# The second MLP product of a two-layer transformer block as three products of scaled fp16 halves

## The chip, the cores and the metric

The kernel runs on one core of one Trainium2 chip, as one launch. The metric is the device time of that core in microseconds (us), 3227.24 as the median of three runs (3226.8 to 3229.04) for the kernel before. The core has five engines that work through instruction queues of their own and meet only at semaphores: TensorE (PE, with its weight loads as PEld), VectorE (DVE), ScalarE (ACT), GpSimd (POOL) and SyncE (SP), which issues the DMAs here.

## The reference

The input x is 4 sequences of 2048 tokens of width 256. First comes an attention stage over the whole sequence, then two layers of local attention and MLP, each stage wrapped in a layer norm and a residual. The change touches the MLP of the layers; `h` is the token-shifted, normalised stream:

```
def _layer(x, wqkv, qs, ksc, wo, lg, lb, w1, b1, w2, b2):
    ...
    x = x + o @ wo
    h = shift_token(x)
    mu = h.mean(-1, keepdims=True)
    var = h.var(-1, keepdims=True)
    h = (h - mu) / jnp.sqrt(var + 1e-05) * lg + lb
    h = h @ w1 + b1
    a, g = jnp.split(h, 2, axis=-1)
    h = a * jax.nn.gelu(g, approximate=False)
    x = x + h @ w2 + b2
    return x
...
for l in range(2):
    x = _layer(x, ...)
```

The hidden width is 682, so `h @ w2` sums over 682 = 5 x 128 + 42 channels and gives 256 columns for each token. All of it is float32 in the reference.

## The kernel before

**Stages.** `phase_a` (the first quarter of the time) does the full attention. `phase_b` does the two layers. It begins with a setup block (L541 to L679) in which SP loads the weights, ScalarE and VectorE split `wqkv`, `wo` and `w1` into a high and a low half, GpSimd scales the rotary tables (L611) and takes a maximum over the partitions (L608), and everyone meets before the main block.

**Slots.** A window is 128 tokens; the two layers together have 128 windows, in 64 pairs. The main block is a software pipeline of slots, one window entering per slot (`slots`, L481; the middle of each layer is a hardware loop of four slots). In slot `s`, an engine runs its part of several stages for different windows: projection and norms of window `s`, scores and softmax of window `s-1`, weighted values and output projection of window `s-2`, the second norm of window `s-3`, and every second slot a piece of the MLP for a pair of windows. In an **even slot** TensorE ends with the first MLP product (L942, 66 matmuls in fp16, already three products of halves); ScalarE applies the gelu (L1013) and VectorE makes `hid` (L1172), six chunks of 128 channels by 256 tokens in float32. In the following **odd slot** TensorE ends with the second MLP product (L953), out of `hid` and `w2` in float32. VectorE adds the residual to it at the start of the next even slot (`layer_output`, L1061).

**What sets the order.** The program text does: each engine's `run` is written out as a fixed order, and an engine that waits for a semaphore holds up all that stands behind. TensorE's order in a slot is: query and key transposes (L845, L852), projections (L867), transposes of the softmax weights (L883), weighted values (L895), scores (L908), output projection (L921), transpose of the next input (L834), and then an MLP product. VectorE's order in an odd slot is: the low halves of query and key (L1096, L1098), second-norm statistics (L1105 to L1109), rotary products (L1039 to L1041, twice, with L1115 and L1118 between), in layer 1 also output statistics (L1068 to L1073), `oT_low` (L1088), eight masked score rows (L1136), `normalise(0)` and `normalise(1)` (L1146, L1149), `xp` (L1160), `normalise(2)`, `keep_hT` (L1024), `normalise(3)`. ScalarE's order there is: L972, L975, the two squares (L979, L981), the copy of v (L984), four copies of transposed weights (L990), the high half of the attention output (L993), eight exponentials (L1000). `oT_low` waits for L993, which waits for L895 of the same slot; the score rows wait for L908; the output projection L921 waits for `oT_low`.

The second product before is one group of float32 matmuls for each window of the pair:

```
pe.wait_ge(hid_ready, HC * (j + 1))
...
for n in range(2):
    for c in range(HC):
        last = nc.tensor.matmul(ps[:, 3, n * D:(n + 1) * D], hid[:, c, n * P:(n + 1) * P], w2[:, ds(layer(2 * j), 1), c, :],
                                start=(c == 0), stop=(c == HC - 1))
last.then_inc(w2_done, 1)
```

## Time and profile before

| | |
|---|---|
| median of three runs | 3227.24 us |
| the profiled execution | 3229.98 us |
| its span, first to last instruction | 3228.2 us |
| PE busy | 3079.6 us, 95% |
| PEld busy | 2590.6 us, 80% |
| DVE busy | 2731.2 us, 85% |
| ACT busy | 1945.7 us, 60% |
| POOL busy | 1872.1 us, 58% |
| PE in the chain that ended last | 71% of the span |

The trace is of one execution. Busy time is an average over phases with different limits, so a stretch of the trace is read for each question. In a row of the timeline the first number is the start, the second the duration, in us from the start of the span; a bracket names the idle time before the row and what ended it. The two MLP products stand in the list of groups as L942 with 4224 matmuls and L953 with 1536, which is 24 for each pair (two records for each float32 matmul in the text).

### The profile page before, as it was taken

What the parts mean: (1) busy time and instruction counts of PE and PEld (TensorE: products, weight loads), DVE (VectorE), ACT (ScalarE), POOL (GpSimd) and SP (SyncE); (2) the same over time, 40 slices, a digit from 0 to 9 for tenths busy, and PEclk for the clock granted to TensorE, in tenths of its full rate; (3) what the DMA queues carried; (4) which work ended last, traced back from release to release, by engine and by line L of the source; (5) the groups of instructions that cost most, each with busy time, mean ns of one, the idle gap of its engine ahead of it and who ended that gap; (6) DMA issues with size and microseconds to landing.
All of it is one profiled execution on the core that took longest, in us unless ns stands there. A gap on an engine that the chain in (4) does not pass through costs nothing.

```text
span 3228.2 us, 86154 instructions
## 1 busy us (share of the span) xinstructions
PE 3079.6 (95%) x25112; PEld 2590.6 (80%) x25112; DVE 2731.2 (85%) x7864; ACT 1945.7 (60%) x4381; POOL 1872.1 (58%) x2307
## 2 busy tenths in 40 slices
PE   6999999994599999999999999999999999999997
PEld 3675848484488888888888888888888888888886
DVE  6878797875688888888888888899999999999995
ACT  5526181622366676666766666666666667676673
POOL 2333434243566666666666666666767767676763
PEclk9999999996799999999999999999999999999999
DMA  1111202015111111111111111122121121211211
GB/s 37 40 59 31 73 19 72 26 63 199 51 45 51 55 49 50 47 53 51 51 49 48 53 49 54 49 52 66 54 61 54 56 64 56 59 54 56 66 56 44
DMA packets 275103, 179.35 MB, mean 56 GB/s; under 512 B 95278, under 2 KB 272914, under 8 KB 274578
## 3 DMA queue, kind: packets, MB, share of 16 engines
q1 hardware_dynamic: 274962, 177.86, 19.0%
q8 instruction: 41, 0.67, 0.1%
q14 instruction: 100, 0.82, 0.1%
HBM read 106.44 MB, written 54.54 MB: 50 GB/s over the span
## 4 chain that ended last, share of the span: by engine, by line
PE 71%; DVE 1%; POOL 1%; issue 1%; ACT 0%; DMA 0%; POOLq 0%; DVEq 0%; SPq 0%; ACTq 0%
PE b_ps L867 16%; PE b_ps L942 14%; PE b_ps L953 10%; PE b_ps L895 7%; PE b_ps L883 7%; PE b_ps L921 6%; PE b_ps L908 6%; PE b_ps L852 2%; PE b_ps L845 2%; PE b_ps L834 1%; POOL b_sq L1188 0%; POOL b_rn L1221 0%; DVE b_probs L1136 0%; DVE b_probs L1149 0%; POOL b_t L1210 0%
## 5 line engine op out<-in xcount | busy, mean ns | idle before, releaser
L1000 ACT ACTIVATE b_probs<-b_probs,b_negmax 128x256 f32<-128x256 f32 x1024 | 505.9, 495 | 78.3 <-DVE b_negmax L1136 77.4
L867 PE MATMUL b_ps<-b_wqkv,b_hT_hi 128*128 128x512 f32 x1536 | 494.5, 403 | 1.0 <-DVE b_hT_lo L1024 1.0
L942 PE MATMUL b_ps<-b_h2T,b_w 128*128 128x256 f16 x4224 | 474.0, 273 | 6.5 <-DMA b_h2T<-b_xh_hl 6.5
L942 PEld LDWEIGHTS b_ps<-b_h2T,b_w 128*128 128x128 f16 x4224 | 414.3, 98 | 55.2 <-DMA b_h2T<-b_xh_hl 6.9
L1188 POOL TENSOR_TENSOR b_sq<-b_sq 128x512 f32<-128x512 f32 (+5 forms) x768 | 418.7, 545 | 61.7 <-ACT b_sq L981 21.6
L1221 POOL TENSOR_TENSOR b_rn<-b_ss_min,b_mhalf 128x16 f32<-128x16 f32 x128 | 377.4, 2948 | 108.8 <-DVE b_ss_min L1048 108.6
L1149 DVE TENSOR_SCALAR b_probs<-b_probs,b_rinv 128x256 f32<-128x256 f32 x1024 | 409.6, 442 | 18.2
L1198 POOL TENSOR_TENSOR b_rstd<-b_var,b_mhalf 128x1 f32<-128x1 f32 x128 | 72.0, 562 | 555.8 <-DVE b_var L1109 555.8
L442 PE MATMUL a_ps<-a_xs,a_E 128*128 128x256 f16 x3072 | 345.2, 273 | 4.1 <-POOL a_xs L233 4.0
L953 PE MATMUL b_ps<-b_w,b_hid 128*128 128x256 f32 x1536 | 342.2, 379 | 1.2 <-DVE b_hid L1172 1.2
L434 PE MATMUL a_ps<-a_xnT 128*128 128x512 f16 x1536 | 339.2, 385 | 3.0 <-ACT a_xnT L382 2.4
L442 PEld LDWEIGHTS a_ps<-a_xs,a_E 128*128 (+1 forms) x3072 | 297.7, 98 | 40.1 <-issue 6.6
L867 PEld LDWEIGHTS b_ps<-b_wqkv,b_hT_hi 128*128 128x128 f32 x1536 | 284.6, 192 | 55.0 <-ACT b_hT_hi L965 1.4
L1136 DVE CUSTOM_DVE_ANT_0 b_probs<-b_ps,b_mask,b_rn 128x256 f32<-128x256 f32 x768 | 324.5, 478 | 0.0
L953 PEld LDWEIGHTS b_ps<-b_w,b_hid 128*128 128x128 f32 x1536 | 286.8, 190 | 37.9 <-DVE b_hid L1172 1.5
L867 PE MATMUL b_ps<-b_wqkv,b_hT_lo 128*128 128x512 f32 x768 | 304.3, 396 | 0.0
L434 PEld LDWEIGHTS a_ps<-a_xnT 128*128 x1536 | 151.8, 99 | 189.2 <-issue 13.0
L990 ACT COPY b_probsT<-b_ps 128x512 f32<-128x512 f32 x512 | 264.0, 611 | 4.7 <-PE b_ps L883 4.6
L1013 ACT ACTIVATE b_gl<-b_ps,b_b,b_w_unit 128x256 f32<-128x256 f32 (+1 forms) x384 | 202.7, 561 | 102.0 <-DVE b_hid L1172 70.0
L895 PE MATMUL b_ps<-b_probsT,b_v 128*64 128x128 f32 x4096 | 251.8, 276 | 0.0
L883 PE MATMUL b_ps<-b_ident_f,b_probs 128*128 128x128 f32 x2048 | 245.9, 273 | 3.5 <-DVE b_xpp L1061 2.2
L883 PEld LDWEIGHTS b_ps<-b_ident_f,b_probs 128*128 128x128 f32 x2048 | 232.7, 142 | 20.1 <-DVE b_xpp L1061 2.5
(133 smaller groups left out, 6507.5 us busy)
## 6 DMA issues: line engine op xcount, KB each, us to landing
b_hx<-xs_dram SPq DMA_DIRECT2D x256, 64.0 KB, 1.9
b_rot<-rot_dram SPq DMA_DIRECT2D x128, 128.0 KB, 2.1
b_xr<-xs_dram SPq DMA_DIRECT2D x128, 128.0 KB, 2.1
xp_dram<-b_xp SPq DMA_DIRECT2D x128, 128.0 KB, 1.7
b_h<-xp_dram SPq DMA_DIRECT2D x256, 64.0 KB, 1.8
a_xn<-in_L_attn_x_dram SPq DMA_DIRECT2D x20, 512.0 KB, 3.8
a_x_res<-in_L_attn_x_dram SPq DMA_DIRECT2D x66, 128.0 KB, 2.1
x_dram<-a_x SPq DMA_DIRECT2D x64, 128.0 KB, 1.7
```

The source lines that it names most:

```text
L434: last = nc.tensor.matmul(ps[:, 4 * u + n, :], xnT[:, a, k, rows], xnT[:, c, k, n * 512:(n + 1) * 512], start=(k == 0 and a == 0 and c == ...
L442: last = nc.tensor.matmul(ps[:, bank, 0:D], E[:, a, j, ds(i * P, P)], xs[:, c, j, :], start=(j == 0 and a == 0 and c == 0), stop=(j == WPB ...
L867: last = nc.tensor.matmul(ps[:, bank, :], hT[:, k, :], wqkv[:, ds(layer(s), 1), part, k, bank * INNER:(bank + 1) * INNER], start=(k == 0 a ...
L883: last = nc.tensor.transpose(ps[:, 3 + p, n * P:(n + 1) * P], probs[:, 2 * p + n // 2, (n % 2) * P:(n % 2 + 1) * P], ident_f[:])
L895: last = nc.tensor.matmul(ps[h * DH:(h + 1) * DH, 7, p * P:(p + 1) * P], v[:, window, (2 * p + h) * DH:(2 * p + h + 1) * DH], probsT[:, p, ...
L942: last = nc.tensor.matmul(ps[:, bank, half * 2 * P:(half + 1) * 2 * P], w1[:, ds(layer(2 * j), 1), wp, k, first:first + P], h2T[:, hp, k, ...
L953: last = nc.tensor.matmul(ps[:, 3, n * D:(n + 1) * D], hid[:, c, n * P:(n + 1) * P], w2[:, ds(layer(2 * j), 1), c, :], start=(c == 0), sto ...
L1000: nc.scalar.activation(probs[:, h, :], probs[:, h, :], ACT.Exp, bias=negmax[:, h:h + 1], scale=-1.0, accum_out=rowsum[:, h:h + 1]).then_in ...
L1136: nc.vector.tensor_tensor_reduce(probs[:, h, :], head_scores(h), which, rn[:, (r - 1) % 2, h:h + 1], ABOVE_ALL, ALU.add, ALU.min, negmax[: ...
L1149: nc.vector.tensor_scalar(probs[:, h, :], probs[:, h, :], rinv[:, h:h + 1], None, ALU.mult).then_inc(probs_ready, 1)
L1188: nc.gpsimd.tensor_tensor(target, target, sq[:, :, width:2 * width], ALU.add).then_inc(ss_halved, 1)
L1221: nc.gpsimd.tensor_tensor(rn[:, r % 2, :], ss_min[:], mhalf[:], ALU.pow).then_inc(rn_ready, 1)
```

## The change

The second product is computed as the first one is: `hid` is multiplied by a power of two and split in a high half (fp16, by ScalarE) and a low half (what is left, fp16, by VectorE), `w2` is split in the setup, and TensorE adds up high x high, high x low and low x high. `PARTS` is ((0, 0), (0, 1), (1, 0)). The result is scaled back where VectorE adds the residual. In the tile `hid_hl` index 0 is the high half and 1 the low one.

```
+HID_PIECES = HC // 2
...
                     if r % 2 == 1 and in_range(2 * j):
-                        pe.wait_ge(hid_ready, HC * (j + 1))
+                        pe.wait_ge(hid_lo, HID_PIECES * (j + 1))
...
                         for n in range(2):
                             for c in range(HC):
-                                last = nc.tensor.matmul(ps[:, 3, n * D:(n + 1) * D], hid[:, c, n * P:(n + 1) * P], w2[:, ds(layer(2 * j), 1), c, :],
-                                                        start=(c == 0), stop=(c == HC - 1))
+                                for a, (hp, wp) in enumerate(PARTS):
+                                    last = nc.tensor.matmul(ps[:, 3, n * D:(n + 1) * D], hid_hl[:, hp, c, n * P:(n + 1) * P],
+                                                            w2[:, ds(layer(2 * j), 1), wp, c, :],
+                                                            start=(c == 0 and a == 0), stop=(c == HC - 1 and a == 2))
...
+                def hid_high(piece, r, pairs, layer):
+                    j = pairs - 2
+                    if r % 2 == 1 and in_range(2 * j):
+                        chunks = slice(2 * piece, 2 * piece + 2)
+                        act.wait_ge(hid_ready, HC * j + chunks.stop)
+                        wait(act, w2_done, j)
+                        nc.scalar.activation(hid_hl[:, 0, chunks, :], hid[:, chunks, :], ACT.Copy, scale=hid_scale[:, ds(layer(2 * j), 1)]).then_inc(hid_hi, 1)
...
+                    hid_high(0, r, pairs, layer)
+                    if in_range(s):
                         act.wait_ge(k_done, s + 1)
...
+                    hid_high(1, r, pairs, layer)
...
+                    hid_high(2, r, pairs, layer)
+                    if in_range(t):
                         act.wait_ge(pv_done, t + 1)
...
-                            nc.vector.tensor_tensor(xpp[:, n, :], ps[:, 3, n * D:(n + 1) * D], xb[:, (r - 6 + n) % 4, :], ALU.add).then_inc(xpp_ready, 1)
+                            nc.vector.scalar_tensor_tensor(xpp[:, n, :], ps[:, 3, n * D:(n + 1) * D], out_unit[:, ds(layer(2 * j), 1)], xb[:, (r - 6 + n) % 4, :],
+                                                           ALU.mult, ALU.add).then_inc(xpp_ready, 1)
...
+                def hid_low(piece, r, pairs, layer):
+                    j = pairs - 2
+                    if r % 2 == 1 and in_range(2 * j):
+                        chunks = slice(2 * piece, 2 * piece + 2)
+                        dve.wait_ge(hid_hi, HID_PIECES * j + piece + 1)
+                        nc.vector.scalar_tensor_tensor(hid_hl[:, 1, chunks, :], hid[:, chunks, :], hid_scale[:, ds(layer(2 * j), 1)], hid_hl[:, 0, chunks, :],
+                                                       ALU.mult, ALU.subtract).then_inc(hid_lo, 1)
...
                     output_stats(pairs - 3, r, layer)
+                    hid_low(0, r, pairs, layer)
+                    hid_low(1, r, pairs, layer)
                     oT_low(s - 2)
...
                     normalise(0)
                     normalise(1)
+                    hid_low(2, r, pairs, layer)
                     t = s - 2
```

In the setup, VectorE now waits for all loads before the maximum is shared, takes the largest absolute value of `w2` (twice 128x1536) and of `b1`, does the low halves of `wqkv` and `wo` ahead of that wait, works out the scales in some ten steps on 128x2 tiles, and makes the low halves of `w2` (twice 128x1536) behind those of `w1`. ScalarE makes the high halves of `w2` in place of scaling it. The mask is loaded in fewer bytes.

On VectorE, the odd slot before, from the second rotary product to the first score rows (L1088 is `oT_low`):

```order
L1039 TENSOR_TENSOR b_t<-b_ps,b_rot 128x512
L1040 TENSOR_TENSOR b_t<-b_ps,b_rot 128x8x32
L1041 TENSOR_TENSOR b_t<-b_ps,b_rot 128x8x32
L1088 TENSOR_TENSOR b_oT<-b_ps,b_oT 128x512
L1128 ISA
L67 REGISTER_ALU
```

and the same place now (L1145 is `hid_low`, L1151 is `oT_low`):

```order
L1093 TENSOR_TENSOR b_t<-b_ps,b_rot 128x512
L1094 TENSOR_TENSOR b_t<-b_ps,b_rot 128x8x32
L1095 TENSOR_TENSOR b_t<-b_ps,b_rot 128x8x32
L1144 REGISTER_ALU
L1145 SCALAR_TENSOR_TENSOR b_hid_hl<-b_hid,b_hid_scale,b_hid_hl 128x512
L1144 REGISTER_ALU
L1145 SCALAR_TENSOR_TENSOR b_hid_hl<-b_hid,b_hid_scale,b_hid_hl 128x512
L1151 TENSOR_TENSOR b_oT<-b_ps,b_oT 128x512
L1193 ISA
```

Two of the three low pieces stand between the rotary products and `oT_low`. The third stands on VectorE behind `normalise(1)` of the same slot, ahead of `xp` (L1226):

```order
L1214 TENSOR_SCALAR b_probs<-b_probs,b_rinv 128x256 x2
L1210 REGISTER_ALU
L1211 RECIPROCAL b_rinv<-b_rowsum 128x2
L1212 REGISTER_ALU
L1214 TENSOR_SCALAR b_probs<-b_probs,b_rinv 128x256 x2
L1144 REGISTER_ALU
L1145 SCALAR_TENSOR_TENSOR b_hid_hl<-b_hid,b_hid_scale,b_hid_hl 128x512
L1223 REGISTER_ALU
L1226 TENSOR_TENSOR b_xp<-b_ps,b_xr 128x256
```

Before, `xp` (L1160) came directly behind the second pair of L1149.

On TensorE, the end of the odd slot now, with the waits (L959 is the output projection, L872 the transpose of the next input, L992 the second MLP product):

```order
L959 MATMUL b_ps<-b_wo,b_oT 128x256 [waits b_v_kept,b_oT_lo]
L959 MATMUL b_ps<-b_wo,b_oT 128x256 x11
L872 MATMUL b_ps<-b_ident_f,b_hx 128x128 [waits b_oT_lo,b_hx_loaded]
L872 MATMUL b_ps<-b_ident_f,b_hx 128x128
L992 MATMUL b_ps<-b_w,b_hid_hl 128x256 [waits b_scores_kept,b_hid_lo]
L992 MATMUL b_ps<-b_w,b_hid_hl 128x256 x35
L883 MATMUL b_ps<-b_ident_f,b_qr 128x128 [waits b_xp_ready,b_v_kept,b_qr_ready]
```

The product stands where it stood; its one wait, ahead of the first of now 36 matmuls, has changed from `hid_ready` to `hid_lo`.

On ScalarE the three high pieces (L1013) stand in the odd slot behind the first square, behind the second square, and behind the four copies of transposed weights (L1042), ahead of the high half of the attention output (L1047):

```order
L1020 CAST b_qT<-b_ps 128x512
L1023 CAST b_kT<-b_ps 128x4x128
L1027 ACTIVATE b_sq<-b_ps 128x512
L1013 ACTIVATE b_hid_hl<-b_hid,b_hid_scale 128x512
L1031 ACTIVATE b_sq<-b_ps 128x512
L1013 ACTIVATE b_hid_hl<-b_hid,b_hid_scale 128x512
L1036 COPY b_v<-b_ps 128x512
```

Nothing else of the main block has moved.

## Rows read from the trace of the kernel before

**Rows 1.** Busy time by stretch, one of layer 0 and one of layer 1.

```profile
core 0: us, PE busy (x) PEld busy (x) DVE busy (x) ACT busy (x) POOL busy (x), PEclk, DMA share, GB/s
1200.00:1400.00 200.00, 200.00 (x1718) 178.52 (x1716) 173.82 (x539) 138.85 (x344) 126.61 (x144) 1.00 0.18 50
2600.00:2800.00 200.00, 200.00 (x1707) 178.38 (x1706) 183.24 (x578) 137.42 (x340) 139.01 (x156) 1.00 0.20 56
```

**Rows 2.** Chain that ended last, in layer 0 (start us, us, what).

```profile
2007.33 7.21 PE b_ps L942 x66
...
2015.41 4.12 PE b_ps L867 x18
2019.53 1.75 PE b_ps L883 x16
...
2024.78 1.63 PE b_ps L921 x12
...
2026.63 5.18 PE b_ps L953 x24
2031.81 0.44 PE b_ps L845 x4
```

**Rows 3.** VectorE's timeline, odd slot of layer 0 (start, duration; idle before, what ended it).

```profile
2023.84 0.69 DVE L1088 TENSOR_TENSOR b_oT<-b_ps,b_oT 128x512 fp32r<-128x512 f32 x1 [1.36 <-ACT b_oT L993]
2024.44 0.47 DVE L1136 CUSTOM_DVE_ANT_0 b_probs<-b_ps,b_mask_now,b_rn 128x256 f32<-128x256 f32 x1
...
2028.68 0.62 DVE L1149 TENSOR_SCALAR b_probs<-b_probs,b_rinv 128x256 f32<-128x256 f32 x2
2029.21 0.42 DVE L1160 TENSOR_TENSOR b_xp<-b_ps,b_xr 128x256 f32<-128x256 f32 x1
```

**Rows 4.** GpSimd's timeline in the same slot.

```profile
2021.92 1.28 POOL L1207 TENSOR_TENSOR b_qr<-b_t 128x512 f32<-128x512 f32 x1
2023.15 1.48 POOL L1188 TENSOR_TENSOR b_sq<-b_sq 128x128 f32<-128x128 f32 x4
2024.59 1.29 POOL L1210 TENSOR_TENSOR b_t<-b_t 128x512 f32<-128x512 f32 x1
2027.12 3.02 POOL L1221 TENSOR_TENSOR b_rn<-b_ss_min,b_mhalf 128x16 f32<-128x16 f32 x1 [1.24 <-DVE b_ss_min L1048]
```

**Rows 5.** ScalarE's timeline in the same slot.

```profile
2019.56 0.59 ACT L984 COPY b_v<-b_ps 128x512 f32<-128x512 f32 x1 [0.77 <-PE b_ps L867]
...
2023.22 0.59 ACT L993 CAST b_oT<-b_ps 128x512 fp32r<-128x512 f32 x1 [1.11 <-PE b_ps L895]
```

**Rows 6.** VectorE's timeline in an odd slot of layer 1.

```profile
2718.67 0.69 DVE L1088 TENSOR_TENSOR b_oT<-b_ps,b_oT 128x512 fp32r<-128x512 f32 x1
...
2724.05 0.42 DVE L1160 TENSOR_TENSOR b_xp<-b_ps,b_xr 128x256 f32<-128x256 f32 x1
```

**Rows 7.** Chain in that slot of layer 1.

```profile
2721.45 5.18 PE b_ps L953 x24
```

**Rows 8.** VectorE's timeline in the setup.

```profile
790.50 3.09 DVE L652 TENSOR_REDUCE p_top<-p_w_f 128x1 f32<-128x2816 f32 x1
...
802.51 11.71 DVE L670 SCALAR_TENSOR_TENSOR b_w<-p_w_f,p_w_scale,b_w 128x2816 f16<-128x2816 f32 x1
...
815.27 3.14 DVE L670 SCALAR_TENSOR_TENSOR b_w<-p_w_f,p_w_scale,b_w 128x2816 f16<-128x2816 f32 x1
```

**Rows 9.** GpSimd's timeline in the setup.

```profile
801.95 9.31 POOL L611 TENSOR_TENSOR p_rot_all<-p_rot_all,p_head_scale 128x4096 f32<-128x4096 f32 x1 [6.76 <-issue]
```

**Rows 10.** TensorE's timeline behind an idle stretch, main block's first slots.

```profile
894.29 0.63 PE L845 MATMUL b_ps<-b_ident_f,b_qr 128*128 128x128 f32 x4 [3.18 <-DVE b_xp L1160]
```

**Rows 11.** TensorE's timeline behind an idle stretch near the end.

```profile
3168.40 3.51 PE L883 MATMUL b_ps<-b_ident_f,b_probs 128*128 128x128 f32 x16 [2.25 <-DVE b_xpp L1061]
```

**Rows 12.** Chain just behind Rows 10, the same 18 matmuls as in Rows 2.

```profile
896.94 6.43 PE b_ps L867 x18
```

**Rows 13.** Busy time and clock (the 0.50) of the stretch of Rows 11.

```profile
3168.40:3171.60 3.20, 3.20 (x15) 3.20 (x16) 1.32 (x5) 1.51 (x3) 1.23 (x2) 0.50 0.68 210
```

More of the change, by code:

```diff
@@ L651, in _ @@
                     dve.wait_ge(w1_gained, KD * (l + 1))
-                    nc.vector.tensor_reduce(top[:, l:l + 1], w1_f[:, l].rearrange("p k n -> p (k n)"), AX.X, ALU.max, apply_absolute_value=True).then_inc(top_ready, 1)
+                    nc.vector.tensor_reduce(top[:, 0, l:l + 1], w1_f[:, l].rearrange("p k n -> p (k n)"), AX.X, ALU.max, apply_absolute_value=True).then_inc(top_ready, 1)
+                dve.wait_ge(loaded, 16 * DMAS)
+                dve.wait_ge(cleared, 4)
+                for l in range(LAYERS):
+                    nc.vector.tensor_reduce(top[:, 1, l:l + 1], w2_f[:, l].rearrange("p c n -> p (c n)"), AX.X, ALU.max, apply_absolute_value=True).then_inc(top_ready, 1)
+                for l in range(LAYERS):
+                    nc.vector.tensor_tensor(b1[:, l, :], ps[:, l, 0:W1_BLOCKS], b1_f[:, l, :], ALU.add).then_inc(bias_added, 1)
+                for l in range(LAYERS):
+                    dve.wait_ge(bias_added, l + 1)
+                    nc.vector.tensor_reduce(top[:, 2, l:l + 1], b1[:, l, :], AX.X, ALU.max, apply_absolute_value=True).then_inc(top_ready, 1)
+                for l in range(LAYERS):
+                    dve.wait_ge(qkv_hi, l + 1)
+                    nc.vector.tensor_tensor(wqkv[:, l, 1], wqkv_f[:, l], wqkv[:, l, 0], ALU.subtract)
+                for l in range(LAYERS):
+                    dve.wait_ge(wo_hi, l + 1)
+                    nc.vector.tensor_tensor(wo[:, l, 1], wo_f[:, l], wo[:, l, 0], ALU.subtract)
                 dve.wait_ge(top_shared, 1)
@@ L656, in _ @@
                 dve.wait_ge(step, 1)
[L657 removed]
+                nc.vector.tensor_scalar(pow2[:].bitcast(I32), top_min[:, 0:2].bitcast(I32), 0x7F800000, None, ALU.bitwise_and).then_inc(step, 1)
                 dve.wait_ge(step, 2)
                 nc.vector.reciprocal(pow2_inv[:], pow2[:]).then_inc(step, 1)
[L660 removed]
@@ L661, in _ @@
-                dve.wait_ge(step, 4)
-                nc.vector.tensor_scalar(w1_scale[:], pow2_inv[:], W1_TOP, None, ALU.mult).then_inc(scale_ready, 1)
-                for l in range(LAYERS):
-                    dve.wait_ge(qkv_hi, l + 1)
-                    nc.vector.tensor_tensor(wqkv[:, l, 1], wqkv_f[:, l], wqkv[:, l, 0], ALU.subtract)
+                nc.vector.tensor_scalar(w1_unit[:], pow2[:, 0], 1.0 / W1_TOP, None, ALU.mult).then_inc(step, 1)
+                nc.vector.tensor_scalar(w2_unit[:], pow2[:, 1], 1.0 / W1_TOP, None, ALU.mult).then_inc(step, 1)
@@ new lines, in _ @@
+                dve.wait_ge(step, 7)
+                nc.vector.tensor_scalar(pre_pow2[:].bitcast(I32), pre_floor[:].bitcast(I32), 0x7F800000, None, ALU.bitwise_and).then_inc(step, 1)
+                dve.wait_ge(step, 8)
+                nc.vector.scalar_tensor_tensor(pre_sq[:], pre_pow2[:], 4.0, pre_pow2[:], ALU.mult, ALU.mult).then_inc(step, 1)
+                dve.wait_ge(step, 9)
+                nc.vector.reciprocal(pre_inv[:], pre_sq[:]).then_inc(step, 1)
+                nc.vector.tensor_scalar(pre_half[:], pre_sq[:], 1.0 / HID_TOP, None, ALU.mult).then_inc(step, 1)
@@ L667, in _ @@
+                dve.wait_ge(step, 11)
+                nc.vector.scalar_tensor_tensor(hid_scale[:], pre_inv[:], HID_TOP, w1_unit[:], ALU.mult, ALU.mult)
+                nc.vector.tensor_tensor(out_unit[:], pre_half[:], w2_unit[:], ALU.mult)
                 dve.wait_ge(scale_ready, 1)
@@ L1167, in run @@
                     if r % 2 == 0 and in_range(2 * j):
-                        wait(dve, w2_done, j)
+                        wait(dve, hid_hi, HID_PIECES * j)
                         for c, bank in enumerate(W1_BANKS):
```

58 lines of the change are left out of this document (35 added, 23 removed).

## The prediction

> **What bounds the kernel now.** I read the busy time by stretches first. In 200 us of layer 0 TensorE is busy for 200.00 us and VectorE for 173.82; in layer 1 it is 200.00 and 183.24 [rows 1]. TensorE sets the pace of the main block and has no hole; VectorE has 26 us of holes in 200, in layer 1 only 17. Then the chain that ended last: in the layers it is TensorE alone, piece after piece [rows 2]. The second MLP product is 5.18 us of a slot [rows 2], so what it saves counts in full, as long as TensorE never has to wait for what the change adds. So the third view is VectorE's timeline in the slot where the product stands [rows 3, 6]: where is VectorE when TensorE reaches the product? TensorE gets there at 2026.63. VectorE is then still in its score rows; it ends the second pair of the normalising steps and starts `xp` at 2029.21, which is 2.58 us later [rows 2, 3]. In layer 1 it is 2724.05 against 2721.45, 2.60 us [rows 6, 7]. The third low piece stands just before `xp`, and the product waits for it.
>
> **The product itself.** Before: 24 records in 5.18 us. Now: 36 fp16 matmuls of 128x256, the form of L942, which takes 7.21 us for 66, that is 0.109 each: 3.93 us. TensorE's work falls by 1.25 us a pair, 80 us over 64 pairs.
>
> **The wait for the third low piece.** A VectorE step of 128x512 with two inputs takes 0.69 us, and the next one starts 0.60 behind its start [rows 3]. The score rows can't start sooner: `oT_low` ends an idle time of 1.36 us on ScalarE's copy, which waited for TensorE's weighted values of that very slot [rows 3, 5]. VectorE is tied to TensorE's place in the slot, so it can't build up a lead. With nothing else late, the third piece ends at 2029.21 + 0.69, some 0.05 pass until TensorE starts, and the product starts 2.58 + 0.74 = 3.32 us later than before. Behind TensorE's wait stands its whole next slot, so the delay is paid in full: 3.32 - 1.25 = 2.07 us longer in layer 0 even if the first two pieces are free.
>
> **The first two low pieces.** They stand ahead of `oT_low`. The room there is 2023.84 minus the end of the rotary product, 1.36 us and a little, and two pieces need 1.20. But they read two tiles in SBUF and GpSimd is at work. In the setup one and the same step, L670, takes 3.14 us alone and 11.71 us when it is issued at 802.51 beside a GpSimd step that runs from 801.95 to 811.26 [rows 8, 9]: 811.26 plus 3.14 is 814.40 and it ended at 814.22, so it stood until GpSimd was through. In the odd slot GpSimd is in `qr` until 2023.20 and then has four short steps in 1.48 us, 0.37 each [rows 4]. I expect: first piece from 2023.20, one short step of GpSimd (0.37), second piece, `oT_low` at 2023.20 + 0.60 + 0.37 + 0.60 = 2024.77, which is 0.93 late. In layer 1 there is no idle time before `oT_low` [rows 6], so both pieces come on top, 1.20 us and about 0.3 of waiting for short steps: 1.5. All of VectorE's slot is late by that, the third piece too; the output projection waits for `oT_low` as well, but that wait lies ahead of the larger one and isn't added.
> Layer 0: 2.07 + 0.93 = 3.0 us a pair. Layer 1: 2.60 + 0.74 + 1.5 - 1.25 = 3.6. Mean 3.3, times 64: 211 us. From both sides: with no waiting for GpSimd at all it is 2.07 and 3.29, 172 us. With the longest plain step, 1.29 us [rows 4], ahead of each piece it is 4.4 and 5.9, 329 us. I take 211, since the neighbours there are the short steps.
>
> **TensorE's clock.** The product starts 3.3 + 0.9 or 1.5 us late, most of it as one hole (in layer 0 4.25 less the 0.7 that TensorE already waits ahead of the output projection: 3.6 us). In this trace TensorE was idle for 2.25 us at the end, and the next 16 transposes took 3.51 us for 1.75, at a granted clock of 0.50, that is 1.2 in place of 2.4 GHz [rows 2, 11, 13]: 1.76 lost. After 3.18 us of idle time the 18 projections took 6.43 for 4.12: 2.3 lost, with a second short idle time between [rows 2, 10, 12]. Now there is such a hole in every pair. Bounds 0 and 2.3 us a pair; I take 1.7, near the row with one hole, and with it 109 us. It falls on the product and the next slot, all on the path.
>
> **ScalarE.** Three pieces of about the size of its 128x512 copies, 0.59 us. The second and third stand where it idles 0.77 and 1.11 us [rows 5]; the first can push the second square by a part of its own length, and GpSimd's sums with it, work that TensorE needs only a slot later, which itself now starts 3 us later. I put it at nothing. If the third one did not fit its hole, `oT_low` would be later by as much; the low pieces cover that too. The scaling in `layer_output` is one operand more in a step of the same size: nothing. GpSimd's own delay by the first two pieces, 2 x 0.60, is hidden in the same way.
>
> **The setup.** L652 takes 3.09 for 2816 elements [rows 8], so the two maxima of `w2` (1536 elements each) take 3.4 us, the two low halves by L670's 3.14 the same, the small steps some 2; the new order also puts the subtractions before the shared maximum, and GpSimd's 9.3 us [rows 9] behind it, where it can again hold VectorE. ScalarE's part changes little. Between 0 and 20; I take 10 us.
>
> **Sum.** 211 + 109 + 10 = 330 us on the profiled execution of 3229.98 (span 3228.2 and 1.8 around it): 3560. It stands 2.7 us over the median of the runs, so 3557; rounded, **3555 us**.
>
> **What a page says against this.** During GpSimd's power step, 2027.12 to 2030.14, VectorE's pair of L1149 took 0.62 us, its usual time [rows 3, 4]: a step that is long on 16 elements does not hold VectorE up. The Trainium skill, in SBUF — State Buffer, section "SBUF: two separate sides", states that a VectorE instruction with two SBUF inputs and a GpSimd instruction that reads SBUF exclude each other for the whole instruction. For L670 the trace agrees. For the power step this trace's pairs do not, though they have one input and not two, so it could still hold for the low piece; that is a rival below.
>
> **Rivals.**
> *The clock stays up.* The wait is there, but TensorE's hole does not cost clock, because work on both sides is dense, while at 894 us the slots had further holes. Against it: 2.25 us was enough once. 3555 - 109 = 3446.
> *The third piece waits for the power step.* With VectorE 0.93 us late, so is the power step: it would run 2028.05 to 2031.07 and the third piece, due at 2030.14, would start 0.93 later. Likewise in layer 1. 64 x 0.93 = 60 us: 3615. For it: L670 and its two inputs. Against it: L1149 beside that very step.
> *Faster: the third piece is in time.* If it is ready by 2026.63, only the saving is left: 3227 - 80 + 10 = 3157. It decides from the point where VectorE comes to the third piece 3.3 us earlier in TensorE's slot than the rows show, say since the product's wait is passed with TensorE's queue still full of older work. What speaks for it is VectorE's holes, 26 us in 200. What speaks against it: the holes lie before `oT_low`, where VectorE waits for TensorE, and none between there and `xp`. Were it half right, with the third piece 1.2 us late, the kernel would come out even.
>
> **How the numbers follow.** Likeliest, wait and clock: 0.62, with its own range 3490 to 3620. Clock stays up: 0.2. Power step: 0.13. The third piece in time: 0.04, and about even: 0.01. The ends: all lower bounds give 3227 + 172 = 3399, all upper ones 3227 + 329 + 147 + 20 = 3723. The range of 8 in 10 takes in the rivals of the clock and the power step and leaves out the corners: 3425 to 3635. A difference under 0.2% (6 us) could not be told from none. Faster 0.04, same 0.01, slower 0.95.
>
> **What the profile of the changed kernel would show.** L992: 36 matmuls a pair, 3.9 us where the clock is full, up to double behind the hole. A wait of TensorE at L992 for VectorE's L1145 of 3 to 4 us in each of some 60 odd slots, the longest entry in the list of waits; PE's share of the span falls from 95% to under 90%. A wait at L959 for L1151 of 0.5 to 1 us in layer 0 and more in layer 1. L1145 of 0.6 to 0.7 us at best, the first two pieces of a slot longer, the third plain. The granted clock at 0.50 behind many of the holes, the mean at about 0.9 in the layers. A pair of slots 4 to 6 us longer, nearly all of it from the odd one's output projection on. Wrong would be: no wait at L992, or the third piece issued before the score rows end; a clock of 1.00 throughout would leave the first rival.

## The result, and the profile after

| | before | changed kernel |
|---|---|---|
| median of the timed runs | 3228.06 us (3226.8 to 3229.04, 4 runs) | 3587.07 us (3585.11 to 3589.63, 4 runs) |
| span of the profiled execution | 3228.2 us | 3587.8 us |
| TensorE busy | 3079.6 us (95%) | 3147.2 us (88%) |
| VectorE busy | 2731.2 us (85%) | 2919.8 us (81%) |

The changed kernel is slower: ratio 1.1113, interval 1.1094 to 1.1132, 359 us more. The forecast was 3555 us with a range of 3425 to 3635; the time lies in it, 32 us above the forecast.

The busy time by stretches, the same two stretches as [rows 1]:

```profile
1200.00:1400.00 200.00, 182.31 (x1601) 158.59 (x1600) 167.38 (x480) 132.09 (x312) 116.09 (x129) 0.96 0.16 45
2600.00:2800.00 200.00, 176.16 (x1510) 151.81 (x1509) 167.69 (x504) 127.13 (x303) 121.80 (x132) 0.94 0.17 49
```

TensorE, without a hole before, now stands for 18 us in 200, in layer 1 for 24. VectorE is busy for a smaller share too (167 against 174 and 183), though it has more to do per pair: it is late, not full. TensorE's waits (waited for: us in total, times, longest):

```profile
PE b_ps L992 <- DVE b_hid_hl L1145: 227.9, 63, 4.6
PE b_ps L959 <- DVE b_oT L1151: 54.4, 63, 2.2
```

These are the two waits that the working asked for, once in each of 63 pairs. In the kernel before each of the two lines waits for VectorE once only: 1.4 us for `oT_low`, 1.2 us for `hid`. The chain that ended last, in one odd slot of layer 0 (it answers to [rows 2]; start, us, what):

```profile
2015.15 0.44 PE b_ps L883 x4
...
2023.86 1.63 PE b_ps L946 x24
...
2030.75 0.76 DVE b_hid_hl L1145
2031.51 0.12 issue
2031.63 5.69 PE b_ps L992 x36
2037.32 0.44 PE b_ps L883 x4
```

Before, this chain was TensorE's alone. Now it leaves TensorE behind the scores, goes through VectorE's score rows and normalisations (left out here) to the third low piece, and comes back at the product. To count how much later the product starts, the timeline is used and not the chain. A piece of the chain begins at the modelled end of the matmul before it, while matmuls overlap: TensorE had issued its next one 0.16 us earlier. Before (L953 is the product, L845 and L852 the first two steps of the next slot):

```profile
2026.47 5.34 PE L953 MATMUL b_ps<-b_w,b_hid 128*128 128x256 f32 x24
2031.65 0.60 PE L845 MATMUL b_ps<-b_ident_f,b_qr 128*128 128x128 f32 x4
2032.09 0.60 PE L852 MATMUL b_ps<-b_ident_f,b_kr 128*128 128x128 f32 x4
```

The slot's first transposes start at 2014.37 before and at 2014.99 now, so the product starts 2026.47 - 2014.37 = 12.10 us into the slot before and 2031.63 - 2014.99 = 16.64 now, which is 4.54 later. VectorE in the same slot, answering to [rows 3]:

```profile
2023.15 2.32 DVE L1145 SCALAR_TENSOR_TENSOR b_hid_hl<-b_hid,b_hid_scale,b_hid_hl 128x512 f16<-128x512 f32 x2
2025.39 0.68 DVE L1151 TENSOR_TENSOR b_oT<-b_ps,b_oT 128x512 fp32r<-128x512 f32 x1
2025.99 0.47 DVE L1201 CUSTOM_DVE_ANT_0 b_probs<-b_ps,b_mask_now,b_rn 128x256 f32<-128x256 f32 x1
...
2030.22 0.61 DVE L1214 TENSOR_SCALAR b_probs<-b_probs,b_rinv 128x256 f32<-128x256 f32 x2
2030.75 0.75 DVE L1145 SCALAR_TENSOR_TENSOR b_hid_hl<-b_hid,b_hid_scale,b_hid_hl 128x512 f16<-128x512 f32 x1
```

and GpSimd beside it, answering to [rows 4]:

```profile
2024.00 2.26 POOL L1254 TENSOR_TENSOR b_sq<-b_sq 128x128 f32<-128x128 f32 x4
2026.21 1.30 POOL L1276 TENSOR_TENSOR b_t<-b_t 128x512 f32<-128x512 f32 x1
2028.74 2.91 POOL L1287 TENSOR_TENSOR b_rn<-b_ss_min,b_mhalf 128x16 f32<-128x16 f32 x1 [1.23 <-DVE b_ss_min L1102]
```

The idle time of 1.36 us ahead of `oT_low` [rows 3] is gone, filled by the two pieces, which need 2.32 us (three in a row take 2.07 in x9 below, where nothing holds them). Counted in both from the chain's start of the slot, `oT_low` starts 2025.39 - 2015.15 = 10.24 us in, and before 2023.84 - 2014.53 = 9.31: 0.93 later. GpSimd's four short steps take 2.26 us in place of 1.48 [rows 4]: the two engines hold each other up. The third piece lies fully inside GpSimd's power step and takes its plain 0.75.

TensorE at the product, and then busy time and clock (third figure from the end) in its first 3.5 us and in the rest:

```profile
2031.63 5.69 PE L992 MATMUL b_ps<-b_w,b_hid_hl 128*128 128x256 f16 x36 [3.61 <-DVE b_hid_hl L1145]
```

```profile
2031.65:2035.15 3.50, 3.50 (x18) 2.53 (x19) 2.99 (x8) 0.00 (x0) 1.77 (x2) 0.53 0.16 52
2035.20:2037.30 2.10, 2.10 (x22) 1.91 (x20) 0.00 (x0) 0.00 (x0) 0.00 (x0) 1.00 0.12 33
```

Behind the hole of 3.61 us the granted clock is 0.53 in the mean of 3.5 us, nearly all of them at the lower level (1.2 GHz), and then 1.00 (2.4 GHz). Here the clock's cost falls on the product alone. In layer 1:

```profile
2699.77 1.47 DVE L1145 SCALAR_TENSOR_TENSOR b_hid_hl<-b_hid,b_hid_scale,b_hid_hl 128x512 f16<-128x512 f32 x2
2701.16 0.68 DVE L1151 TENSOR_TENSOR b_oT<-b_ps,b_oT 128x512 fp32r<-128x512 f32 x1
...
2706.52 0.75 DVE L1145 SCALAR_TENSOR_TENSOR b_hid_hl<-b_hid,b_hid_scale,b_hid_hl 128x512 f16<-128x512 f32 x1
```

```profile
2690.34 0.45 PE b_ps L883 x4
...
2707.40 5.73 PE b_ps L992 x36
```

By the timeline the slot begins at 2690.18, so the product starts 17.22 us in; before it was 2721.29 - 2709.19 = 12.10. That is 5.12 later. `oT_low` is 2701.16 - 2690.34 = 10.82 in by the chain's start of the slot, before 2718.67 - 2709.36 = 9.31 [rows 6]: 1.51 later.

For the experiments one more measure is used: the length of a pair, as the mean of 28 differences between starts of the second product, in layer 0 and in layer 1. It is 36.56 and 36.41 us before, 41.80 and 42.29 after.

### The profile page after: what moved, and what is told of

Its sections match the earlier page's. It is cut to its first block, busy times and chain, and to the rows that moved or that the text cites. A ratio compares the mean times of both kernels' runs of the same rounds, so it can differ in the third digit from the quotient of the medians.

```text
span 3587.8 us, 88553 instructions
## 1 busy us (share of the span) xinstructions
PE 3147.2 (88%) x25880; PEld 2585.8 (72%) x25880; DVE 2919.8 (81%) x8074; ACT 2071.3 (58%) x4573; POOL 1921.5 (54%) x2307
## 4 chain that ended last, share of the span: by engine, by line
PE 56%; DVE 13%; issue 5%; POOL 1%; ACT 1%; DVEq 0%; DMA 0%; POOLq 0%; ACTq 0%; SPq 0%
PE b_ps L905 13%; PE b_ps L980 12%; PE b_ps L992 11%; PE b_ps L933 6%; PE b_ps L921 5%; DVE b_probs L1201 4%; PE b_ps L946 4%; PE b_ps L959 3%; DVE b_hid_hl L1145 2%; DVE b_probs L1214 2%; PE b_ps L883 1%; PE b_ps L890 1%; DVE b_oT L1151 1%; DVE b_negmax L1201 0%; DVE b_t L1093 0%
## 5 line engine op out<-in xcount | busy, mean ns | idle before, releaser
L992 PE MATMUL b_ps<-b_w,b_hid_hl 128*128 128x256 f16 x2304 | 387.6, 350 | 227.9 <-DVE b_hid_hl L1145 227.9
L992 PEld LDWEIGHTS b_ps<-b_w,b_hid_hl 128*128 128x128 f16 x2304 | 283.5, 125 | 329.1 <-issue 207.5
L1254 POOL TENSOR_TENSOR b_sq<-b_sq 128x512 f32<-128x512 f32 (+5 forms) x768 | 467.7, 609 | 60.0 <-ACT b_sq L1031 19.7
L1287 POOL TENSOR_TENSOR b_rn<-b_ss_min,b_mhalf 128x16 f32<-128x16 f32 x128 | 374.7, 2927 | 137.8 <-DVE b_ss_min L1102 137.6
L1214 DVE TENSOR_SCALAR b_probs<-b_probs,b_rinv 128x256 f32<-128x256 f32 x1024 | 430.8, 462 | 18.2
L1020 ACT CAST b_qT<-b_ps 128x512 fp32r<-128x512 f32 x128 | 75.2, 587 | 469.1 <-PE b_ps L883 467.5
L1159 DVE TENSOR_TENSOR b_qT_low<-b_ps,b_qT 128x512 fp32r<-128x512 f32 x128 | 88.4, 691 | 249.1 <-ACT b_qT L1020 240.8
L1042 ACT COPY b_probsT<-b_ps 128x512 f32<-128x512 f32 x512 | 263.7, 609 | 2.8 <-PE b_ps L921 2.7
L959 PE MATMUL b_ps<-b_wo,b_oT 128*128 128x256 f32 x1536 | 216.6, 290 | 54.4 <-DVE b_oT L1151 54.4
```

The lines of the kernel that those rows point to most:

```text
L959: last = nc.tensor.matmul(ps[:, 2, 0:D], oT[:, op, p, :], wo[:, ds(layer(t), 1), wp, p, :], start=(p == 0 and a == 0), stop=(p == HP - 1 a ...
L992: last = nc.tensor.matmul(ps[:, 3, n * D:(n + 1) * D], hid_hl[:, hp, c, n * P:(n + 1) * P], w2[:, ds(layer(2 * j), 1), wp, c, :], start=(c ...
L1042: nc.scalar.copy(probsT[:, p, :], ps[:, 3 + p, :]).then_inc(pT_kept, 1)
L1214: nc.vector.tensor_scalar(probs[:, h, :], probs[:, h, :], rinv[:, h:h + 1], None, ALU.mult).then_inc(probs_ready, 1)
L1254: nc.gpsimd.tensor_tensor(target, target, sq[:, :, width:2 * width], ALU.add).then_inc(ss_halved, 1)
L1287: nc.gpsimd.tensor_tensor(rn[:, r % 2, :], ss_min[:], mhalf[:], ALU.pow).then_inc(rn_ready, 1)
```

## The experiments

Each was timed beside the kernel before (3227 to 3228 us in every comparison). "Slower by" is against that.

| run | time, us | ratio and interval | pair in layer 0, 1, us | product, us |
|---|---|---|---|---|
| changed kernel | 3587.07 | 1.1113 [1.1094, 1.1132] | 41.80, 42.29 | 5.95, 6.25 |
| x1_no_low | 3219.06 | 0.997 [0.9957, 0.9982] | 36.31, 35.97 | 4.09, 4.09 |
| x2b_filler | 3463.16 | 1.073 [1.0712, 1.0747] | 39.89, 40.11 | 4.10, 4.10 |
| x3_by_piece | 3380.28 | 1.0467 [1.045, 1.0485] | 38.60, 38.99 | 4.97, 4.97 |
| x4_third_early | 3352.98 | 1.0384 [1.0366, 1.0401] | 37.95, 38.57 | 4.09, 4.45 |
| x11_third_only | 3492.19 | 1.0815 [1.0797, 1.0833] | 40.59, 40.25 | 5.58, 5.58 |
| x12_first_two | 3287.19 | 1.0182 [1.0165, 1.0199] | 37.24, 37.18 | 4.09, 4.09 |
| x5_spread | 3446.19 | 1.0676 [1.0658, 1.0693] | 39.94, 39.95 | 4.43, 4.43 |
| x7_no_low_floor | 3410.35 | 1.0567 [1.0549, 1.0584] | 39.84, 38.82 | 4.10, 4.10 |
| x8_before_floor | 3389.22 | 1.0506 [1.0488, 1.0523] | 38.63, 39.69 | 5.45, 5.45 |
| x9_behind_scores | 3406.95 | 1.0551 [1.0533, 1.0569] | 39.28, 39.17 | 4.10, 4.22 |
| x10_xp_first | 3408.47 | 1.0556 [1.0538, 1.0573] | 39.07, 39.40 | 4.10, 4.10 |
| x13_third_behind_scores | 3375.98 | 1.0452 [1.0434, 1.0469] | 38.59, 39.00 | 4.09, 4.09 |

The product's time is from the start of its first matmul to the modelled end of its last; it includes waits inside (x3). By this measure the product before takes 5.35 us. From its first start to the start of what follows it is 0.16 to 0.17 less: 5.18 before, 3.93 for 4.09.

**x1_no_low.** Only the product, without the low pieces that VectorE has to make.

```diff
-pe.wait_ge(hid_lo, HID_PIECES * (j + 1))
+pe.wait_ge(hid_hi, HID_PIECES * (j + 1))
-... hid_hl[:, hp, c, n * P:(n + 1) * P] ...
+... hid_hl[:, 0, c, n * P:(n + 1) * P] ...
-hid_low(0, r, pairs, layer)
-hid_low(1, r, pairs, layer)
-hid_low(2, r, pairs, layer)
```

> This kernel leaves the low half of the hidden activations out: VectorE makes no low pieces in the main block, and TensorE runs its 36 fp16 matmuls with the high half throughout, behind ScalarE's high pieces. Theory (the loss is TensorE's wait for VectorE's third low piece, the delay that the first two put on oT_low, and the clock behind the hole): all three go, the product takes 3.9 us at full clock, and the time is 3228 - 80 for the product + 12 for the longer setup = 3160, up to 3180 if GpSimd's chain for the keys is now the one that is late. Rival 1 (36 matmuls with 36 weight loads cost 5.4 to 5.7 us in themselves): 3228 + 64 x 0.4 + 12 = 3265.

Measured 3219.06. Two things follow. The low pieces are the whole loss: 368 us of it hang on three VectorE steps of 0.75 us per pair. But the gain is about a tenth of what the product saves, and this expectation missed by 39 to 59 us. Of the expected saving of 80, setup takes 12, as expected (the first hx transposes start at 835.55 us, before at 823.39). The product saves 5.35 - 4.09 = 1.26 us a pair, and the pair shortens by 0.25 in layer 0 and 0.44 in layer 1. TensorE's waits show the main taker:

```profile
PE b_ps L890 <- POOL b_kr L1289: 39.3, 66, 6.2
```

and the chain that ended last in layer 0 is no longer TensorE's but GpSimd's:

```profile
2008.54 0.34 POOL b_sq L1251
...
2009.49 1.25 POOL b_t L1273
...
2011.98 3.01 POOL b_rn L1284
2015.07 1.04 POOL b_kr L1289
```

With the product shorter, TensorE comes to the transposes of `kr` before GpSimd has multiplied it. GpSimd isn't full (busy 517 us of 800 in layer 0); it is the chain of steps up to `kr` that is long. The trace of the kernel before holds this already, off TensorE's row:

```profile
2030.22 1.04 POOL L1226 TENSOR_TENSOR b_kr<-b_t,b_rn 128x512 f32<-128x512 f32 x1
```

There `kr` is ready at 2031.26 and TensorE starts to transpose it at 2032.09, 0.83 us later. A product shortened by 1.25 us uses up this room.

Of the 39.3 us, 14.2 in 4 waits stand in the kernel before too; new are 25 us, 0.4 a pair. Since an idle time is counted from the modelled end of the matmuls before, the wait costs more than that. From the transposes before `kr` (L845, here L883) to the end of those of `kr`, start to start, a pair takes 0.76 us more than before in layer 0 and 0.65 in layer 1 (means of 28 pairs). The projections take 0.20 and 0.16 us a pair more by the same count. Together this leaves 1.25 - 0.96 = 0.29 and 1.25 - 0.81 = 0.44 us of the saving, where 0.25 and 0.44 were measured.

**x2b_filler.** The hole filled, to see the clock's share.

```diff
-pe.wait_ge(hid_lo, HID_PIECES * (j + 1))
+pe.wait_ge(hid_ready, HC * (j + 1))
 if in_range(s - 1):
     pe.wait_ge(scores_kept, HEADS * (s - 1) + BANK_READ[3])
+for _ in range(28):
+    nc.tensor.matmul(ps[:, 3, 0:D], w1[:, 0, 0, 0, 0:P], w1[:, 0, 0, 0, 0:D], start=True, stop=True)
+pe.wait_ge(hid_lo, HID_PIECES * (j + 1))
```

> In the changed kernel TensorE idles 3.6 us in every odd slot before the second product (line 992), and the granted clock then falls to 0.50 once per pair; the product takes 5.4 to 5.7 us where 36 matmuls at full clock take 3.93. Here 28 matmuls whose result is thrown away (some 3.05 us at full clock, one pass 128x256) stand in that hole, behind the wait for the hidden activations and ahead of the wait for the low pieces; the output is as before. Theory (the fall of the clock is a cost of its own, beside the wait): clock 1.00 throughout the block loop, product 3.9 to 4.0 us, some 1.7 us less in each of 63 pairs, near 3480 us. Rival (the clock's fall costs nothing that the wait would not cost anyway): 3587 within 10 us. If the filler runs past the arrival of the third piece, up to 0.5 us per pair is given back, so 3480 to 3515.

Measured 3463.16: 17 us below the 3480 expected, and 124 us less than the changed kernel with 28 more matmuls per pair. The trace of TensorE there:

```profile
2019.11 3.22 PE L990 MATMUL b_ps<-b_w 128*128 128x256 f16 x28
2022.81 4.11 PE L995 MATMUL b_ps<-b_w,b_hid_hl 128*128 128x256 f16 x36 [0.48 <-DVE b_hid_hl L1148]
```

The hole that remains is 0.48 us, the product takes 4.11, and the granted clock is 1.00 in both stretches of the block loop looked at (1200 to 1400 and 2600 to 2800 us). So the fall of the clock is a cost of its own, 124 us or 1.9 us a pair, and with the clock up the low pieces still cost 3463.16 - 3219.06 = 244 us, by TensorE's two waits.

**x3_by_piece.** The product in order of the chunks, with a wait per piece.

```diff
+nc.tensor.matmul(ps[:, 3, :], zero_h[:], w1[:, 0, 0, 0, 0:2 * D], start=True, stop=False)
-for n in range(2):
-    for c in range(HC):
+for c in range(HC):
+    if c % 2 == 0:
+        pe.wait_ge(hid_lo, HID_PIECES * j + c // 2 + 1)
+    for n in range(2):
```

> TensorE takes the product chunk by chunk for both windows, and waits for each low piece apart: 24 of the 36 matmuls (2.6 us) can run before the third piece. One matmul of zeros over both windows opens the sum (0.2 us). VectorE's and ScalarE's order is that of the changed kernel. Theory: the third piece is as late as before, but behind it stand 12 matmuls, 1.3 us at full clock, and not 36 at a lowered one, 5.5 us: 4.2 us less in each of 63 pairs, 3587 - 265 = 3322; the hole is 0.8 us in layer 0 and the clock stays at 1.00. Rival 2 (VectorE has become the bound by the amount of its work, 1.9 us more a pair, wherever it stands): VectorE's work is the same, so 3587 or little less.

Measured 3380.28, 58 above the expectation. The clock stays up and the wait inside the product falls to 45.1 us in 63 waits. The one for `oT_low` stays (61.2 us, 54.4 in the changed kernel), and new ones stand around it: 22.2 us for `qT_low`, 18.1 for `hT_lo`, all steps of VectorE.

**x4_third_early.** The third piece with the first two, ahead of `oT_low`.

```diff
 hid_low(1, r, pairs, layer)
+hid_low(2, r, pairs, layer)
 oT_low(s - 2)
...
 normalise(1)
-hid_low(2, r, pairs, layer)
```

> Only the third low piece moves, to behind the second one, ahead of oT_low. Theory: the wait at the product goes, and the one at the output projection grows from 0.9 us on average to about 1.8 (0.66 for the piece and a short step of GpSimd). Per pair 1.8 - 1.25 = 0.55 more than before the change: 3228 + 12 + 35 = 3275 if holes of 1.8 us leave the clock alone, 3380 if they lower it as the long one does. Rival 2 (amount of VectorE's work): 3587 or little less. Rival 3 (GpSimd's steps hold all three pieces up, 1.3 us each): 3228 + 12 + 64 x 2.5 = 3400.

Measured 3352.98, the best of the versions that compute the whole result and 234 us better than the changed kernel, yet 78 above what I expected:

```profile
2039.71 3.03 DVE L1145 SCALAR_TENSOR_TENSOR b_hid_hl<-b_hid,b_hid_scale,b_hid_hl 128x512 f16<-128x512 f32 x3
2042.67 0.68 DVE L1151 TENSOR_TENSOR b_oT<-b_ps,b_oT 128x512 fp32r<-128x512 f32 x1
```

Three pieces take 3.03 us, and TensorE's wait for `oT_low` is 104.0 us in 63 waits, 1.65 each, close to the 1.8 that I had expected. So the hold-up beside GpSimd is not what I missed. It is first of all the wait for `kr`: 42.8 us in 57 waits, of which 14.2 stand in the kernel before. x1 has it as well (39.3), so it comes from the shorter product and not from the place of the third piece. In layer 1 the clock falls at times too: the product takes 4.45 us there, and the granted clock is 0.98 from 2600 to 2800 us.

**x11_third_only and x12_first_two.** The two places of the change apart.

```diff
 # x11: no hid_low(0), hid_low(1); chunks 0 to 3 use the high half
+... hid_hl[:, hp if c >= 4 else 0, c, n * P:(n + 1) * P] ...
 # x12: no hid_low(2); chunks 4 and 5 use the high half
+... hid_hl[:, hp if c < 4 else 0, c, n * P:(n + 1) * P] ...
```

> The changed kernel without its first two low pieces (chunks 0 to 3 multiply the high half three times; their low half is left out); the third piece stands where it does in the changed kernel and TensorE waits for it before the whole product. Theory: this piece carries most of the loss. The wait before line 992 (227.9 us there) and the fall of the clock stay, the wait for oT (54 us) goes: 3587 - 54 = 3533 us. Rival (the first two are the larger part, since the third comes behind them): 3400 us or less.

> The changed kernel with the first two low pieces and without the third (chunks 4 and 5 multiply the high half three times; their low half is left out). Theory: what is left is that oT_low, and with it the score rows, the floor step and GpSimd's kr, come 0.9 us (layer 0) to 1.5 us (layer 1) later, in a loop that without low pieces already waits for kr: 3219 + 64 x (0.9 to 1.5) = 3277 to 3315 us, near 3296, and the clock stays 1.00. Rival (the pieces beside GpSimd's halving steps are held and hold these, 2.3 us for two): 3340 us or more.

Over the 3219.06 of x1_no_low, the first two pieces cost 68 us and the third 273, in sum 341 of the 368 that all three cost. x12 came out as expected (3287 for 3277 to 3315), and its waits are those of the theory: 54.6 us for `oT_low`, and 47.5 for `kr` (39.3 in x1 without any low piece). x11 is 41 below the expectation: without the first two pieces the whole slot of VectorE is earlier, so the third is too, and the clock loses less (the product takes 5.58 us, 5.95 and 6.25 with all three). One VectorE step of 0.75 us in the wrong place costs 273 us, since TensorE waits for it 3.5 us a time (217.9 us in 63 waits) and pays some 1.5 us of clock on top (5.58 against 4.09).

**x7_no_low_floor and x8_before_floor.** x1_no_low had shown GpSimd's power step as the bound. It waits for VectorE's floor step on the squared norms, which stands ahead of the seventh score row. Here it stands ahead of the third: x7 without low pieces, x8 the kernel before with this one change.

```diff
 for p in range(HP):
-    if p == HP - 1:
+    if p == 1:
         floor_norms(s)
```

> As the kernel without low pieces (36 matmuls, each of a high half; the low half of the hidden activations is left out), with the floor step on the squared norms ahead of the third score row instead of the seventh, so that GpSimd's power step starts about 0.8 to 1.3 us earlier. Theory (after the shorter product GpSimd's chain to kr bounds the loop and ate the saving): the wait of line 890 for kr, 39 us in 66 waits, goes and the kernel takes 3180 to 3190 us. Rival (something else holds, kr was only the last of several): 3205 to 3219 us.

> The kernel before with nothing changed but the floor step on the squared norms, four score rows earlier as in the run beside it. Theory: TensorE is never idle there and kr is not waited for, so 3228 us within 0.2%. Rival (the floor step is worth something by itself): 3190 to 3215 us.

Both theories and both rivals fell: x8 is 162 us slower than the kernel before, x7 191 us slower than x1_no_low. VectorE and GpSimd in x8, an even slot of layer 0:

```profile
2007.60 1.17 DVE L1048 TENSOR_SCALAR b_ss_min<-b_sq 128x16 f32<-128x16 f32 x1
...
2011.30 0.62 DVE L1149 TENSOR_SCALAR b_probs<-b_probs,b_rinv 128x256 f32<-128x256 f32 x2
2011.83 0.16 DVE L1146 RECIPROCAL b_rinv<-b_rowsum 128x2 f32<-128x2 f32 x1
2012.03 1.47 DVE L1149 TENSOR_SCALAR b_probs<-b_probs,b_rinv 128x256 f32<-128x256 f32 x2
```

```profile
2007.44 1.29 POOL L1210 TENSOR_TENSOR b_t<-b_t 128x512 f32<-128x512 f32 x1
2008.93 3.04 POOL L1221 TENSOR_TENSOR b_rn<-b_ss_min,b_mhalf 128x16 f32<-128x16 f32 x1 [0.19 <-DVE b_ss_min L1048]
2012.05 1.04 POOL L1226 TENSOR_TENSOR b_kr<-b_t,b_rn 128x512 f32<-128x512 f32 x1
```

The floor step has 16 elements. Issued beside GpSimd's L1210, it ends at 2008.77, when L1210 has ended (2008.73): it stood for a whole GpSimd step. The pair of normalisations issued while GpSimd multiplies to `kr` ends at 2013.50 and takes 1.47 in place of 0.62. Over the whole run the floor step takes 1062 ns in the mean against 205 before, and L1149 516 against 442: 128 x 0.86 + 1024 x 0.074 = 186 us more of VectorE's time. In the kernel before the floor step falls behind L1210 and the first three pairs of normalisations start beside the power step, where they take 0.62 us; only the fourth meets `kr` and takes 1.35. That order is worth 162 us.

**x5_spread.** Low pieces ahead of the fifth and the seventh score row and behind the last one, the product of x3, and the floor step ahead of the fifth row.

```diff
 for p in range(HP):
-    if p == HP - 1:
+    if p == HP - 2:
         floor_norms(s)
+    if p >= 2:
+        hid_low(p - 2, r, pairs, layer)
...
+hid_low(2, r, pairs, layer)
```

> The same fp16 product, taken piece by piece (a zero matmul opens the sum, TensorE waits for one piece at a time); no low piece stands ahead of oT_low: pieces 0 and 1 stand among the score rows, piece 2 right behind them, and the small floor step on which GpSimd's power step waits is two rows earlier. The output is unchanged. If the loss lies in where the pieces stand (they hold oT_low, and the third comes after two normalisations), nearly all of it goes: the kernel without low pieces took 3219 us, the zero matmul adds some 0.2 us per pair (14 us), the earlier floor step takes up to 39 us of the wait for kr, and the 2.3 us of the pieces are hidden where TensorE has scores and output projection to do: 3195 to 3260, near 3225 us. Rival (the 2.3 us of VectorE time are themselves the cost, wherever they stand): VectorE is 2.3 us later per pair at hT_lo and the q product waits for it: 3219 + 64 x 2.3 = 3366 us.

Measured 3446.19, 80 us above even the rival. The run changes two things, and x8 shows that the earlier floor step alone is a loss (it takes 1.22 us in the slot at 2037.58), so nothing about the pieces follows from it. The next two runs leave the floor step where it was.

**x9_behind_scores and x10_xp_first.** All three pieces behind the score rows, beside the power step; x10 in addition with the sum `xp` ahead of the normalisations.

```diff
-hid_low(0, r, pairs, layer)
-hid_low(1, r, pairs, layer)
 oT_low(s - 2)
 ...                               # score rows
+hid_low(0, r, pairs, layer)
+hid_low(1, r, pairs, layer)
+hid_low(2, r, pairs, layer)
```

> The same fp16 product piece by piece (a zero matmul opens the sum), all three low pieces right behind the score rows, none ahead of oT_low, and the floor step on the norms left where it was. The output is unchanged. Theory (the cost lies where the pieces stand): oT_low and the score rows are as without low pieces, the pieces run beside GpSimd's power step, which does not hold them; behind them the first two normalisations meet GpSimd's multiplication to kr and are held by about 1 us, and the sum xp, for which TensorE's next transposes wait, is 2.3 to 3.3 us later than without low pieces. TensorE's product starts behind the first piece, so it ends some 1.0 us later than without low pieces, and xp holds it some 1 us more: 3219 + 64 x (1.0 to 2.0) = 3285 to 3350, near 3310 us; clock 1.00. Rival (the 2.3 us are lost wherever they stand): 3366 us or more.

> As the run beside it, with the sum xp ahead of all normalisations and hT_lo behind the first one. The output is unchanged. Theory: TensorE waits for xp and hT_lo no longer; what is left is the late first piece, 3219 + 64 x 1.0 = 3283 us, if the four normalisations, now some 3 us later, are still in time for the transposes of the next slot. Rival: VectorE has no room left (83 to 92% busy before, plus 2.3 us per 36 us), the late normalisations hold TensorE's transposes of probs or the hidden activations of the even slot: 3320 us or more, no better than the run beside it.

Measured 3406.95 and 3408.47: x9 is 57 above the end of its range, and x10 gains nothing on it, as its rival had it. In x9:

```profile
2043.78 2.07 DVE L1150 SCALAR_TENSOR_TENSOR b_hid_hl<-b_hid,b_hid_scale,b_hid_hl 128x512 f16<-128x512 f32 x3
2045.77 0.15 DVE L1217 RECIPROCAL b_rinv<-b_rowsum 128x2 f32<-128x2 f32 x1
2045.96 1.44 DVE L1220 TENSOR_SCALAR b_probs<-b_probs,b_rinv 128x256 f32<-128x256 f32 x2
```

```profile
2043.21 2.91 POOL L1292 TENSOR_TENSOR b_rn<-b_ss_min,b_mhalf 128x16 f32<-128x16 f32 x1 [0.92 <-DVE b_ss_min L1107]
2046.20 1.04 POOL L1297 TENSOR_TENSOR b_kr<-b_t,b_rn 128x512 f32<-128x512 f32 x1
```

The pieces pass the power step without a hold (0.69 each), the normalisation behind them meets `kr` and is held (1.44), both as expected. But TensorE is through with the matmul of zeros at 2042.9 and the first piece ends at 2044.5: 110.7 us of waiting in 63 waits, and it waits for `hT_lo` (34.9) and `qT_low` (21.4) as well.

**x13_third_behind_scores.** x3 with the third piece ahead of the normalisations.

> As the run by piece (zero matmul opens the sum, one wait per piece, 3380 us), with the third low piece right behind the score rows instead of behind the first two normalisations, beside GpSimd's power step. The output is unchanged. Theory (the third piece is late by the two normalisations ahead of it): the wait of the second product, 45.1 us in 63 waits in the run by piece, goes, and nothing else comes later than there, since the same steps stand ahead of xp and hT_lo: 3380 - 45 = 3335 us. Rival (the normalisations, now 0.75 us later, meet GpSimd's multiplication to kr, which holds them, so the sum xp and hT_lo come later): no gain or a loss, 3380 us or more.

Its edit moves one line, `hid_low(2, r, pairs, layer)`, from behind `normalise(1)` to behind the score rows. Measured 3375.98, 4 us better than x3 where 45 were expected; the pairs are the same to 0.01 us. The wait in the product is gone, 36 matmuls run through in 4.09 us:

```profile
PE b_ps L961 <- DVE b_oT L1156: 60.9, 63, 1.5
...
PE b_ps L907 <- DVE b_hT_lo L1083: 37.5, 55, 1.0
PE b_ps L892 <- POOL b_kr L1297: 29.5, 60, 6.2
```

In its place are waits right behind the product, for `hT_lo` (37.5 us, 18.1 in x3) and `kr` (29.5, 14.2 in x3). That is the rival. The waits point to what sets the pace once the third piece is in time: the way through `oT_low`, the score rows, the floor step, the power step and `kr`, and VectorE's own steps up to `hT_lo`. TensorE can wait in the product or behind it. No run takes one of these two ways out by itself.

## Why the prediction came out right

- **The bound and the place of the wait.** Right. 63 waits at line 992 for the third low piece, one a pair, of 3.6 us in the mean; TensorE's share of the span went from 95% to 88%.
- **The product, 3.93 us.** Right: by start to start it is 5.18 us before and 3.93 in x1. The 4.09 to 4.11 us of the table and of x2b's row count the tail of the last matmul as well, as the 5.35 before does.
- **The third piece, 3.32 us late.** Right in kind, a little small: the product started 4.54 us later in layer 0 and 5.12 in layer 1, forecast were 3.32 + 0.93 = 4.25 and 2.60 + 0.74 + 1.5 = 4.84. Of the missing 0.29 and 0.28, 0.16 is a misreading: I took 2026.63, where the product's piece of the chain begins [rows 2], for the moment when TensorE gets to it, and that was 2026.47. Another 0.08 is in the slot's projections.
- **The first two pieces, 0.93 and 1.5.** Measured 0.93 and 1.51. x12 shows them by themselves: pairs longer by 0.93 (36.31 to 37.24) and 1.21 us. In layer 1 the size was right for a partly wrong reason: I counted 0.3 us of waiting by VectorE, and there it was mostly GpSimd that was held (L1145 1.47 for two there, 2.32 in layer 0).
- **The clock, 1.7 us a pair, 109 us.** Right in kind, a little small: x2b measured 124 us. I had taken the row with one hole of 2.25 us [rows 11]; the hole here is 3.61. The 1.7 was a choice between 0 and 2.3, so its closeness is in part luck.
- **The first rival (the clock stays up, 3446).** x2b is the case made real, at 3463.
- **The power step as a hold-up (3615).** Refuted: the third piece lies inside L1287 with 0.75 us, and three in a row in x9 with 0.69 each. For this the Trainium skill states, in SBUF — State Buffer, section "SBUF: two separate sides", that VectorE with two SBUF inputs and GpSimd reading SBUF exclude each other for the whole instruction. For GpSimd's 128x128 steps the trace agrees (two pieces in 2.32 us, four GpSimd steps in 2.26 for 1.48), for the power step it does not; the measurement decides.
- **Faster, from a third piece in time (3157).** Its condition was tried and its price was wrong. x13 has the piece in time and takes 3376, and even without any low piece the kernel takes 3219, not 3157. The working treated TensorE as the only engine with a claim on the pair's length, and so it booked the product's saving in full. x1 shows that the way to `kr` allowed little less than 36 us a pair. The forecast did not suffer: with the product 4.5 us late, TensorE comes to `kr` after it is ready, and the changed kernel has no more of this wait (14.1 us in 4) than the kernel before. The working says of GpSimd's sums that TensorE needs them only a slot later, but it put no number on how early they were.
- **ScalarE at nothing, setup at 10.** The high pieces take some 0.7 us (0.71 and 0.77 in the slot at 2015); x1 has them all and shows no wait for them but one of 2.7 us. Setup took 12. Its L700, 2 elements wide, stood for 8.73 us beside a GpSimd step on 128x4096, as the forecast had it for a step in this place.

The 32 us that the forecast was short are, per pair and roughly: 0.16 by the misreading above, 0.2 in the clock (x2b), and 0.16 in the projections (4.20 against 4.12 in the chain, twice), 33 us over 64 pairs. Why the projections take 0.08 us more I did not find; x1 and x2b have the 4.20 as well.

The sum of the loss as the runs give it: 124 us is the clock (x2b), 83 the difference to x3, where TensorE takes the pieces one by one, and 4 the third piece's place once that is so (x13); 157 remain up to x1. Some 14 of them are the matmul of zeros that x3 and x13 have and x1 has not (0.22 us a pair). The rest goes with the 2.3 us of VectorE work per pair, and no place that was tried made it cheap (x4, x9, x10 and x13 lie between 134 and 189 over x1); whether another place would is open. The saving of the product gives back 9. No version that makes the low halves on VectorE came near the kernel before; the best is x4 with 3353. Whether GpSimd or the idle part of ScalarE could make them was not tried.
